# Centring every tile on VectorE, all low halves of Wq on VectorE, first loads on two queues

## The reference

```
xn  = (x - mean(x)) / sqrt(var(x) + 1e-5)            # per row
q   = xn @ Wq.T + bq, of which heads 0, 4, 8, ... are used (8 of 32, 128 wide)
s   = elu(q) + 1
r   = (s @ M[head]) / (s . z[head] + 1e-6)
out = x + repeat(r, 4 heads) @ Wo.T + xn @ (w * w_scale) + b
```

## Time and profile before

| | before |
|---|---|
| three runs, median (lowest to highest) | 246.52 us (246.44 to 246.63) |
| the profiled execution | 246.23 us |
| its span, first to last instruction | 244.4 us |
| mean granted clock of TensorE | 1.000 |
| PE busy | 236.9 us, 97% |
| DVE busy | 176.0 us, 72% |
| ACT busy | 119.8 us, 49% |
| POOL busy | 113.5 us, 46% |

### The profile page before, as it was taken

How to read it: one execution, slowest core, us unless ns; L and a number is a source line. 1 busy time by engine, 2 the same in 40 slices (tenths; PEclk the granted TensorE clock), 3 DMA queues, 4 the chain that set the end, 5 groups by cost and what they waited for, 6 DMA issues and landing times.

```text
span 244.4 us, 3386 instructions
## 1 busy us (share of the span) xinstructions
PE 236.9 (97%) x1030; PEld 186.6 (76%) x1030; DVE 176.0 (72%) x261; ACT 119.8 (49%) x276; POOL 113.5 (46%) x113
## 2 busy tenths in 40 slices
PE   6899899999999899999999999999999999999995
PEld 2477688887777578888888888888888888788885
DVE  3839995988998739978587594958666678983331
ACT  3663545629639824655463526346463747341110
POOL 2694743755272615563615326263404629667400
PEclk9999999999999999999999999999999999999999
DMA  6999999999270111424251525222122223245441
GB/s 237 405 415 408 396 232 216 215 216 210 71 247 14 49 48 50 129 54 123 53 168 49 168 52 168 60 80 83 34 53 70 54 75 107 76 134 146 114 169 51
DMA packets 21842, 34.83 MB, mean 142 GB/s; under 512 B 5185, under 2 KB 13121, under 8 KB 20673
## 3 DMA queue, kind: packets, MB, share of 16 engines
q1 hardware_dynamic: 19200, 26.63, 33.0%
q0 software_dynamic: 1376, 6.82, 13.3%
q10 hardware_dynamic: 1248, 1.18, 1.6%
HBM read 22.02 MB, written 4.19 MB: 107 GB/s over the span
## 4 chain that ended last, share of the span: by engine, by line
PE 83%; DVE 7%; ACT 5%; issue 2%; DMA 1%; DVEq 0%; ACTq 0%
PE attn_ps L787 13%; PE attn_ps L789 13%; PE attn_ps L788 13%; PE q_ps L787 9%; PE q_ps L789 9%; PE q_ps L788 9%; PE dense_ps L789 5%; PE dense_ps L787 5%; PE dense_ps L788 5%; ACT s L447 2%; PE attn_ps L851 2%; DMA x<-in_x 1%; DVE stats L557 1%; DVE wd_lo L612 1%; DVE q_ps L626 1%
## 5 line engine op out<-in xcount | busy, mean ns | idle before, releaser
L314 POOL TENSOR_TENSOR e_and_sz<-s,z_b 128x512 f32<-128x512 f32 x32 | 41.7, 1330 | 40.6 <-DVE den L638 40.4
L447 ACT ACTIVATE s<-s,rden 128x128 f32<-128x128 f32 x128 | 39.2, 389 | 40.4 <-DVE rden L642 40.4
L787 PE MATMUL attn_ps<-P_hi,aT_hi 128*128 128x512 f32 (+1 forms) x128 | 50.3, 393 | 0.9 <-DVE P_lo L617 0.8
L789 PE MATMUL attn_ps<-P_hi,aT_lo 128*128 128x512 f32 (+1 forms) x128 | 49.7, 388 | 0.0
L788 PE MATMUL attn_ps<-P_lo,aT_hi 128*128 128x512 f32 (+1 forms) x128 | 49.7, 388 | 0.0
L787 PE MATMUL q_ps<-WqT_hi,xT_hi 128*128 128x512 f32 x104 | 42.2, 406 | 0.9 <-DVE s L633 0.6
L789 PE MATMUL q_ps<-WqT_hi,xT_lo 128*128 128x512 f32 x104 | 40.6, 390 | 0.0
L788 PE MATMUL q_ps<-WqT_lo,xT_hi 128*128 128x512 f32 x104 | 40.5, 390 | 0.0
L284 POOL TENSOR_TENSOR xT<-xT,mean_b 128x512 f32<-128x512 f32 x14 | 20.0, 1431 | 38.4 <-ACT mean_b L396 36.0
L626 DVE SCALAR_TENSOR_TENSOR q_ps<-q_ps,rstd,bq_b 128x512 f32<-128x512 f32 x28 | 21.0, 753 | 20.6 <-PE q_ps L789 20.6
L787 PEld LDWEIGHTS attn_ps<-P_hi,aT_hi 128*128 128x128 f32 x128 | 24.0, 188 | 7.4 <-DVE P_lo L617 1.2
(11 more groups left out here) (82 smaller groups left out, 366.0 us busy)
## 6 DMA issues: line engine op xcount, KB each, us to landing
x<-in_WoT POOLq DMA_DIRECT2D x6, 1024.0 KB, 10.2
x<-in_x SPq DMA_DIRECT2D x16, 256.0 KB, 5.0
xT<-in_xT SPq DMA_DIRECT2D x16, 256.0 KB, 5.1
aT<-s SPq DMA_DIRECT2D x124, 32.0 KB, 1.8
out<-x SPq DMA_DIRECT2D x15, 256.0 KB, 2.3
MT<-s SPq DMA_DIRECT2D x96, 32.0 KB, 1.9
x<-in_WoT SPq DMA_DIRECT2D x2, 1024.0 KB, 14.0
s<-in_WqT SPq DMA_DIRECT2D x3, 512.0 KB, 6.7
```

Of the source, the lines that this page charges most:

```text
L314: nc.gpsimd.tensor_tensor(sz_eps[:, :, h * D // 2:(h + 1) * D // 2].rearrange("p g (j c) -> p j g c", j=2), by_quarter(sbuf_s[:, t % SRING ...
L447: last = nc.scalar.activation(a_g, a_g, ACT.Copy, scale=rden[:, t % 2, g:g + 1])
L787: nc.tensor.matmul(out, x_hi, w_hi, start=start, stop=False)
L789: return nc.tensor.matmul(out, x_lo, w_hi, start=False, stop=stop)
```

## The change

DVE centres every tile from `mean_ps`; `mean_b`, `copy_mean` and POOL's `center` are gone. DVE makes both halves of each `WqT_lo` chunk; POOL's part of that is gone. POOL's list keeps its order otherwise, without those entries. The first loads are shared out: x of tile 0 is cut by partitions over SP and ACT, the two halves of Wq chunk 0 too, and ACT issues tile 1. The first products of PE come in another order, `product_P(7)` moves ahead of `product_dense(7)`, and the first `product_attn` waits for the last `P_lo` only at its last head. In the tail ACT copies `aT_hi(t)` before it issues its share of the next spread.

```diff
 SP
-            load_x(0)
+            sp.dma_start(x[0:P // 2, 0, :], x_d[0][0:P // 2]).then_inc(x_in[0], 16)
             load_xT(0)
+            sp.dma_start(WqT_raw[:, 0, HALF:], WqT_d[0, 0][:, HALF:]).then_inc(wq_first_in[1], 16)
             load_wq(1)
-            load_x(1)
-            load_xT(1)
             load_wq(2)
             load_x(2)
+            load_wq(3)
             load_xT(2)
-            load_wq(3)
 POOL
             rstd_of(0)
-            split_wq_lo(0)
-            split_wq_lo(1)
             rstd_of(1)
-            split_wq_lo(2)
             rstd_of(2)
-            split_wq_lo(3)
-            center(2)
             scale_w()
...
             rstd_of(3)
-            center(3)
             add_wo(1, 0)
             add_wo(1, 1)
             rstd_of(4)
-            center(4)
             rstd_of(5)
             times_z(0, 0)
             add_wo(2, 0)
...
 ACT
-            for h in range(2):
-                act.dma_start(WqT_raw[:, 0, halves(h)], WqT_d[0, 0][:, halves(h)]).then_inc(wq_first_in[h], 16)
+            act.dma_start(x[P // 2:P, 0, :], x_d[0][P // 2:P]).then_inc(x_in[0], 16)
+            act.dma_start(WqT_raw[:, 0, :HALF], WqT_d[0, 0][:, :HALF]).then_inc(wq_first_in[0], 16)
+            act.dma_start(x[:, 1, :], x_d[1]).then_inc(x_in[1], 16)
+            act.dma_start(xT[:, 1, :, :].rearrange("p k r -> p (k r)"), xT_d[1]).then_inc(xT_in[1], 16)
...
-            copy_mean(2)
             cast_w(0)
+            copy_xT_hi(2)
             cast_w(1)
-            copy_xT_hi(2)
...
             make_a(2)
-            copy_mean(8)
+            copy_P_hi(5)
             make_a(3)
...
             for t in range(FIRST_SHARED + 1, T):
+                copy_aT_hi(t)
                 if t + 1 < T:
                     spread_group(t + 1)
-                copy_aT_hi(t)
 DVE
+            def center(t):
+                dve.wait_ge(mean_filled, t + 1)
+                dve.wait_ge(xT_in[t], 16)
+                nc.vector.tensor_tensor(xT[:, t % XRING, :, :], xT[:, t % XRING, :, :],
                                         mean_ps[:, 0:P].unsqueeze(1).to_broadcast([P, K, P]),
                                         ALU.subtract).then_inc(xc_by_dve, 1)
...
+            split_wq_lo(2, 0)
+            split_wq_lo(2, 1)
             moments(2)
+            split_wq_lo(3, 0)
+            split_wq_lo(3, 1)
+            center(2)
             split_xT_lo(2)
             scale_w()
             moments(3)
             add_bias(0, 0)
             add_bias(0, 1)
             split_wd_lo(0)
+            center(3)
             split_wd_lo(1)
...
             add_dense(0)
+            center(4)
             moments(5)
...
             add_dense(1)
+            center(5)
             make_s(2, 0)
...
             for t in range(LEAD, T):
...
                 add_dense(t)
+                if t + 2 < T:
+                    center(t + 2)
 PE
             def spread_mean(t):
                 pe.wait_ge(meanvar_ready, t + 1)
-                if 1 <= t <= 2:
+                if t >= 1:
                     pe.wait_ge(xc_by_dve, t + 1)
-                elif t >= 3:
-                    pe.wait_ge(mean_copied, t - 2)
...
             def product_attn(t):
-                pe.wait_ge(P_lo_ready, G)
+                if t == 0:
+                    pe.wait_ge(P_lo_ready, G - 1)
...
+                    if t == 0 and g == G - 1:
+                        pe.wait_ge(P_lo_ready, G)
...
                 if t == LEAD:
                     product_P(6)
-                product_dense(t, 0, K // 2)
-                if t == LEAD:
                     product_P(7)
-                product_dense(t, K // 2, K)
+                product_dense(t)
```

More of the change, by code:

```diff
@@ L357, in _ @@
             add_wo(2, 1)
-            center(5)
             rstd_of(6)
@@ L363, in _ @@
             add_wo(3, 1)
-            center(6)
             times_z(2, 0)
@@ L367, in _ @@
             rstd_of(7)
-            center(7)
             times_z(3, 0)
@@ L372, in _ @@
             rstd_of(8)
-            center(8)
             for t in range(LEAD, T):
@@ L380, in _ @@
                     rstd_of(t + 2)
-                    center(t + 2)
             times_z(T - 1, 0)
@@ L391, in _ @@
         def _(act):
[L392 to L397, removed]
             def copy_first_xT_hi(j):
@@ L404, in copy_xT_hi @@
             def copy_xT_hi(t):
[L405 to L410, removed]
+                act.wait_ge(xc_by_dve, t + 2)
+                if t >= HRING:
+                    act.wait_ge(dense_filled, t - HRING + 1)
                 nc.scalar.activation(xT_hi[:, t % HRING, :, :], xT[:, t % XRING, :, :], ACT.Copy
@@ L596, in split_xT_lo, with split_wq_lo @@
                                         xT_hi[:, t % HRING, :, :].bitcast(F32), ALU.subtract).then_inc(xT_lo_ready, 1)
[L598 to L601, removed]
+            def split_wq_lo(k, h):
+                cols = halves(h)
+                dve.wait_ge(wq_hi_ready, 2 * k + h + 1)
+                nc.vector.tensor_tensor(WqT_lo[:, k, cols], WqT_raw[:, k, cols], WqT_hi[:, k, cols].bitcast(F32),
+                                        ALU.subtract).then_inc(wq_lo_ready, 1)
             def scale_w():
@@ L668, in _ @@
             nc.vector.memset(warm[:], 0.0).then_inc(warm_set, 1)
-            moments(0)
-            split_wq_lo(0)
+            statistics(0)
+            mean_and_variance(0)
             center_first(0)
+            split_wq_lo(0, 0)
+            split_first_xT_lo(0)
             center_first(1)
-            split_first_xT_lo(0)
+            split_wq_lo(0, 1)
+            statistics(1)
+            mean_and_variance(1)
+            split_wq_lo(1, 0)
+            center(1)
+            split_wq_lo(1, 1)
             split_first_xT_lo(1)
[L675 to L678, removed]
             split_xT_lo(1)
+            variance_eps(0)
+            variance_eps(1)
+            split_wq_lo(2, 0)
+            split_wq_lo(2, 1)
             moments(2)
-            split_wq_lo(3)
+            split_wq_lo(3, 0)
+            split_wq_lo(3, 1)
+            center(2)
             split_xT_lo(2)
@@ L716, in _ @@
             add_bias(4, 1)
+            center(6)
             denominator(1)
@@ L730, in _ @@
             turn_blocks(1)
+            center(7)
             add_dense(5)
@@ L742, in _ @@
             split_P_lo(4)
+            center(8)
             split_aT_lo(0)
@@ L753, in _ @@
                     split_P_lo(6)
+                if t == LEAD:
+                    split_P_lo(7)
                 turn_blocks(t - BEHIND - 1)
                 if t == LEAD:
-                    split_P_lo(7)
+                    split_xT_lo(t + 1)
                 make_s(t, 0)
-                if t + 1 < T:
+                if LEAD < t < T - 1:
                     split_xT_lo(t + 1)
@@ L830, in product_q, with product_dense @@
                 last.then_inc(q_filled, 1)
-            def product_dense(t, first=0, end=K):
-                if t >= 1 and first == 0:
+            def product_dense(t):
+                if t >= 1:
                     pe.wait_ge(dense_added, t)
-                for k in range(first, end):
+                for k in range(K):
                     if t == 0:
@@ L839, in product_dense @@
                                         wd_hi[:, k, :], wd_lo[:, k, :], k == 0, k == K - 1)
-                if end == K:
-                    last.then_inc(dense_filled, 1)
+                last.then_inc(dense_filled, 1)
             def product_P(g):
@@ L875, in _ @@
             hi_lo(0, 0, 0)
+            lo_hi(0, 0, 0)
             hi_hi(0, 1, 0)
-            lo_hi(0, 0, 0)
             lo_hi(0, 1, 0)
@@ L880, in _ @@
             hi_hi(0, 0, 1)
+            lo_hi(0, 0, 1)
+            spread_mean(1)
             hi_hi(0, 1, 1)
-            lo_hi(0, 0, 1)
             lo_hi(0, 1, 1)
-            spread_mean(1)
             hi_lo(0, 0, 1)
+            hi_hi(1, 0, 0)
+            hi_lo(1, 0, 0)
+            hi_hi(1, 1, 0)
+            hi_lo(1, 1, 0)
             hi_lo(0, 1, 1)
@@ L888, in _ @@
             lo_hi(0, 0, 2)
[L889 to L893, removed]
+            lo_hi(1, 0, 0)
+            lo_hi(1, 1, 0)
+            for h in range(2):
+                hi_hi(1, h, 1)
+                hi_lo(1, h, 1)
+                lo_hi(1, h, 1)
             spread_mean(2)
```

35 lines of the change are left out of this document (4 added, 31 removed).

## The result

The changed kernel is slower: ratio 1.0192 to the kernel before, 95% interval 1.0159 to 1.0224, on a median of 246.48 us; that makes 251.2 us, where 250.7 was forecast. The profiled execution took 250.4 us, span 248.6 (before 246.23 and 244.4).

A forecast was written before the change was run, and what follows sets the result against it. PE was taken to bound the kernel. +5.2 us for the late `product_dense(2)` less 1.0 for the wait at the first `product_attn` gave +4.2 on 246.23, so 250.4; the median, 0.29 above, 250.7 us; range 244.4 to 253.0.

The forecast's parts named there:

- The deciding step: Freed POOL issues `add_wo(1, 0)` at 22.1; x of tile 5 lands at 39.0, making `product_dense(2)` 5.2 us late.
- The start: First loads and products: x of tile 0 on both queues gains 0.6 us; `product_q(2, 0)` comes about 0.9 us earlier.
- the count of DVE's work without POOL: Up to `product_q(3, 0)`: DVE's instructions, unhindered by POOL, bring it from 30.45 to 28.25, a gain of 2.2 us.
- Three further terms: Before `product_dense(2)`: issue at 22.1 with landing at 39.0, 4.85 us of DVE work after it, and no clock loss.
- The same row of work as before, 4.85 us: DVE's work from `moments(5)` to `add_dense(1)`, after x of tile 5 lands, put `product_dense(2)` at 43.95.
- the likeliest case: x of tile 5 lands at 39.0, `product_dense(2)` starts at 43.95; 250.7 us, spanning 249.7 to 251.7; chance 0.48.
- the third rival, *part of it: Tile 5 lands between 34 and 37, `product_dense(2)` starts between 39 and 42; 245.7 to 248.7 us; chance 0.09.
- the clock's rival: TensorE's clock halves while PE stands before `product_dense(2)`, whose 12 matmuls cost 2.7 us more: 253.4 us; chance 0.08.
- The rest: Wait at first `product_attn` goes, worth 1.0 us; centring on DVE in the loop and the tail's swap cost nothing.
- The first rival: Transfers start no earlier; PE waits at `product_P(0)`, giving back 1.6 of 2.2 us: 244.9 us; chance 0.24.

The follow-up runs named there:

- e1_hold: The changed kernel with POOL holding the first `add_wo` until x of tile 4 has landed; 245.97 us, ratio 0.9977 to the kernel before.
- e9_before_wo_earliest: The kernel before with the first two `add_wo` moved ahead of `rstd_of(3)` on POOL; 257.31 us, ratio 1.0426 to the kernel before.
- e4_x5_first: The changed kernel with x and xT of tile 5 loaded ahead of z and b; 251.44 us, ratio 0.9989 to the kernel before.
- e2_old_loads: The changed kernel with the first loads of the kernel before put back; 254.03 us, ratio 1.0308 to the kernel before.
- e12_changed_again: The changed kernel run once more, unaltered, for its spread; 253.62 us, ratio 1.0256 to the kernel before.
- e6_late_only: The kernel before with only the change's edits around 80 to 90 us; 245.84 us, ratio 0.9975 to the kernel before.
- e8_combined: The changed kernel with the old first loads, first `add_wo` held until x of tile 4 landed, `product_P(0)` one place later; 244.45 us, ratio 0.9919.
- e5_before_early_wo: The kernel before with the first two `add_wo` moved ahead of `center(3)` on POOL; 247.72 us, ratio 1.0042 to the kernel before.

## Why the prediction came out as it did

**The deciding step was right.** Freed of centring, POOL issued `add_wo(1, 0)` early, x of tile 5 came late, and `product_dense(2)` with it. Taking that issue back (e1_hold) takes the slowdown away; making it early in the kernel before (e9_before_wo_earliest) makes one. The Trainium skill (DMA: Bandwidth & Descriptors, Queues, rings and completion order) has the engines take turns between queues by packets; the trace agrees and gives the price, 146 packets against 144. By the same count the landing could have been estimated: one load of 256 KB in 5.6 us (e4_x5_first), for each that is still to come at the first packet, at most until the two transfers end (39.0 in e2_old_loads, where x of tile 5 landed at 39.3).

**The start was mis-sized, in sign.** "x of tile 0 is moved by both queues", 0.6 us earlier: its statistics began 0.21 earlier, but ACT had the first half of Wq only at 6.64 (4.38 before), and the first product came at 7.63 (7.21 in e12_changed_again) instead of 6.1. The other part of the step, the count of DVE's work without POOL, came out near with the old loads, for which it was not made: `product_q(2, 0)` at 19.35 and `product_q(3, 0)` at 28.11, where 19.7 and 28.25 were forecast. In the changed kernel the 2.2 us at `product_q(3, 0)` were 0 in one profile and 1.6 in the other.

**Three further terms were off and cancelled.** The late start put the issue at 24.80 instead of 22.1, and the landing at 35.8 instead of 39.0 (in e2_old_loads, at 22.07: 39.3). "The same row of work as before, 4.85 us" on DVE took 6.4 us to `product_dense(2)` in all four colliding profiles of the changed kernel's lists (35.79 to 42.17 here): x of tile 5 releases POOL's `times_z` too, so that it runs against `split_xT_lo(4)`, 2.14 us instead of 0.69. The Trainium skill (SBUF — State Buffer, SBUF: two separate sides) has a cause for that: a DVE instruction with two SBUF inputs and a GpSimd one that reads SBUF exclude each other at a shared port for the whole instruction; the trace agrees, 0.69 us alone (e1_hold), 2.14, 3.53 and 4.24 beside POOL, though no run here moves POOL's instruction alone. And the clock, set aside as a rival with 0.08, fell in every profile in which PE stood for a late x unfilled; it belonged to the likeliest case. (The Trainium skill, TensorE: Matmul & The Clock Gate, Part 1: The HAM clock gate, has it drop to half after idleness; the trace agrees, 0.50 in e2_old_loads.) So `product_dense(2)` was 1.8 us earlier than forecast, the clock cost 1.8 more, and 250.4 was met by luck: the mechanism was right, the sum was not.

The profiled execution is in fact nearer to the third rival, *part of it*: z and b were past (29.1 and 30.1), x of tile 5 landed at 35.8 (34 to 37 there), and `product_dense(2)` came at 42.17 (39 to 42 there). That rival's upper end, 248.7, lacks only the clock's 1.8. The likeliest case, with its landing at 39.0, is what e2_old_loads and e12_changed_again show, and there the clock comes on top: e12_changed_again, the same kernel, has a ratio of 1.0256, 252.8 us by the same measure that gave 251.2. The slower executions (253.05 to 256.32) lie around and above the 253.4 of the clock's rival; the one of them that has a profile, 255.37, had its landing at 39.8 and a granted clock of 0.50 from 42 to 50 us.

**The rest was right.** The wait at the first `product_attn` went, for 1.0 us (e6_late_only). In the loop centring on DVE is covered: from 100 to 240 us PE is busy for 139.93 of 140 us before and after. The first rival's wait at `product_P(0)` is real (1.63 us in e1_hold): had the issue stayed in time, the start's gain would have been given back there, as the forecast of 244.9 said; e1_hold gave 245.97, with 0.9 us won at `product_dense(2)` instead of 2.2.

## What to carry to other kernels

An engine that is relieved moves every instruction behind it forward, its transfers too; look up which loads are still in the queue at that moment, and count packets rather than bytes to see who gets the engines (146 against 144 here, for four times the bytes). An issue that must be neither early nor late is better bound to the load it must follow than to the work that happens to stand ahead of it. Price a stand of PE with the clock that it loses, and a late DVE instruction with the POOL instruction that the same event releases.

## What was not expected of the hardware

- After the stand at 4.6 to 5.2 us the first products of e8_combined ran 0.43 us apart until about 10 us, though the windows give 1.00 as granted clock there; with a stand of 0.46 the changed kernel's did not, and with 0.96 those of the kernel before didn't either, but with 0.77 those of e5_before_early_wo did. What decides is open.
- While both transfers run, one load of 256 KB lands every 5.6 us (z at 33.4, b at 38.9, x of tile 6 at 44.6 in e4_x5_first; b at 34.2, x of tile 5 at 39.8 in e12_changed_again), otherwise one in about 0.7 us (z at 28.3, b at 29.0, x of tile 5 at 29.7 before).
- `split_xT_lo` on DVE doesn't only wait out one POOL instruction: in e9_before_wo_earliest it took 4.24 us beside two, with an issue between them.
